# Row maxima added by ScalarE and GpSimd in two attention blocks, and a causal mask added by VectorE in a third

## The reference, cut to what matters

```python
# L1_attn: multi-query, causal; one key/value head of width 16 for all 16 query heads
scores = einsum('bqhd,bkd->bhqk', q, k) / 16 ** 0.5
scores = where(triu(ones(s, s), k=1), -inf, scores)
out = einsum('bhqk,bkd->bqhd', softmax(scores), v) @ o_w.T + o_b
# L2_attn: causal, head width 128
logits = einsum('bthd,bThd->bhtT', q, k) * rsqrt(128)
logits = logits - 1e10 * (1 - (i >= j))
out = (softmax(logits) @ v).reshape(B, T, 2048) @ w_o + b_o
# L2_xattn: head width 16, q against 240 keys of the context and, apart, against 16 more
ctx = _attn(q, k, v) + _attn(q, k_dca, v_dca)
```

## Time and profile before

| | us |
|---|---|
| median of 3 runs | 2208.23 |
| the profiled execution | 2212.03 |
| its span, first to last instruction | 2210.0 |
| TensorE (PE) busy | 1885.6 (85%) |
| VectorE (DVE) busy | 1228.7 (56%) |
| ScalarE (ACT) busy | 787.7 (36%) |
| GpSimd (POOL) busy | 258.7 (12%) |
| mean granted TensorE clock | 0.917 of full speed |

### The profile page before, as it was taken

The page is one execution under the profiler, slowest core; times in us unless marked ns, Lnnn a source line. Parts: engine busy times, 40 slices in busy tenths (PEclk is TensorE's granted clock), DMA queues, the critical chain, the costliest instruction groups (busy, mean ns, idle before and its releaser), DMA issues.

```text
span 2210.0 us, 25454 instructions
## 1 busy us (share of the span) xinstructions
PE 1885.6 (85%) x9078; PEld 1198.9 (54%) x9078; DVE 1228.7 (56%) x2789; ACT 787.7 (36%) x1864; POOL 258.7 (12%) x244
## 2 busy tenths in 40 slices
PE   5684776988669599999898678999998899998698
PEld 3451222555555366666665445555555577777355
DVE  5738998746664444444476685333334666665221
ACT  4215444302342133333344322333333455554111
POOL 2711000000104300000000200000000322220111
PEclk9796877989869799999989889999999999999799
DMA  3001000000442200000000213000002000002210
GB/s 149 1 5 53 0 0 20 1 29 1 188 188 89 96 1 1 1 1 0 4 36 1 100 54 134 0 1 1 0 1 102 15 1 1 1 1 96 85 34 13
DMA packets 17371, 83.13 MB, mean 38 GB/s; under 512 B 3136, under 2 KB 10052, under 8 KB 13152
## 3 DMA queue, kind: packets, MB, share of 16 engines
q1 hardware_dynamic: 11168, 71.35, 8.2%
q0 software_dynamic: 2944, 8.03, 1.2%
q10 hardware_dynamic: 3136, 2.13, 0.3%
HBM read 73.23 MB, written 8.81 MB: 37 GB/s over the span
## 4 chain that ended last, share of the span: by engine, by line
PE 72%; DVE 16%; issue 6%; ACT 3%; POOL 3%; DMA 1%; POOLq 0%; DVEq 0%; SPq 0%; ACTq 0%
PE bank L136 58%; PE bank L141 8%; PE bank L3535 4%; DVE space L795 2%; PE bank L3557 2%; DVE space L784 2%; DVE space L1369 1%; DVE space L3049 1%; DMA space<-in_L_attn 1%; DVE space L178 1%; POOL space L625 1%; POOL space L639 1%; DVE space L272 0%; DVE space L189 0%; ACT space L1551 0%
## 5 line engine op out<-in xcount | busy, mean ns | idle before, releaser
L136 PE MATMUL bank<-space 128*128 128x256 f32 (+16 forms) x6734 | 1453.8, 417 | 73.7 <-ACT space L822 10.3
L136 PEld LDWEIGHTS bank<-space 128*128 128x128 f32 (+7 forms) x6734 | 886.2, 178 | 593.8 <-issue 394.1
L141 PE MATMUL bank<-consts,space 128*128 128x128 f32 (+1 forms) x1602 | 253.5, 299 | 170.7 <-DVE space L189 50.0
L141 PEld LDWEIGHTS bank<-consts,space 128*128 128x128 f32 (+1 forms) x1602 | 201.8, 153 | 236.8 <-issue 123.6
L136 PE MATMUL bank<-space,consts 128*128 128x512 f32 (+2 forms) x150 | 96.2, 769 | 58.5 <-DVE space L790 49.0
L197 POOL TENSOR_TENSOR space<-space,consts 128x4 f32<-128x4 f32 x22 | 24.9, 1132 | 684.8 <-DVE space L184 684.8
L2633 POOL TENSOR_TENSOR space<-space,consts 128x4 f32<-128x4 f32 x64 | 68.6, 1071 | 218.2 <-DVE space L2564 218.2
L2428 ACT ACTIVATE space<-bank,space 128x256 f32<-128x256 f32 x128 | 59.5, 470 | 95.7 <-DVE space L2382 95.7
L2382 DVE TENSOR_REDUCE space<-bank 128x2 f32<-128x512 f32 x64 | 44.1, 688 | 86.9 <-PE bank L136 86.8
L136 PEld LDWEIGHTS bank<-space,consts 128*128 128x128 f32 (+1 forms) x150 | 30.2, 227 | 104.1 <-DVE space L790 70.4
L3535 PE MATMUL bank<-space 128*128 x176 | 80.7, 603 | 3.1 <-DVE space L3685 1.6
(11 more groups left out here) (350 smaller groups left out, 1948.3 us busy)
## 6 DMA issues: line engine op xcount, KB each, us to landing
space<-in_L_ffn SPq DMA_DIRECT2D x13, 2048.0 KB, 11.9
space<-in_L_attn SPq DMA_DIRECT2D x10, 2048.0 KB, 13.4
space<-in_L_xattn SPq DMA_DIRECT2D x4, 2048.0 KB, 10.0
expert_results<-space SPq DMA_DIRECT2D x16, 128.0 KB, 3.6
space<-expert_results SPq DMA_DIRECT2D x8, 256.0 KB, 4.7
space<-in_L_xattn SPq DMA_DIRECT2D x1, 1919.0 KB, 19.8
space<-in_L_xattn SPq DMA_DIRECT2D x1, 1536.0 KB, 6.2
space<-in_L_attn SPq DMA_DIRECT2D x1, 1074.5 KB, 4.9
```

The source lines that it names most:

```text
L136: return self.nc.tensor.matmul(out, lhsT, rhs, start=first, stop=last, skip_group_check=True)
L141: return self.nc.tensor.transpose(out, src, eye)
```

## The change

In the pass of maxima of both `MultiQuery` and `TwoContexts`, the adds of batches 0, 1 and 2 leave VectorE. ScalarE copies each of the two turned banks into a buffer `spare` in `space` and signals `row_kept`; GpSimd adds the buffer to the queries and signals `q_done`. A turn bank is free once it is copied. ScalarE waits with the next batch's copies until GpSimd has added the last one's. The last batch's adds stay with VectorE under a signal of their own, `last_q_done`, which the first mixing product now waits for instead of all of `q_done`. In `Causal` the mask product goes; the two score products now begin their own sums; and VectorE adds the mask to the two diagonal blocks in PSUM ahead of the two row maxima, with a wait between.

```diff
-    def mask_rows(self, bank):
-        out = bank.rearrange("p (a b) -> p a b", b=P)[:, 0::3, :]
-        return self.mm(out, self.ident_bf, repeat(self.mask_bf, 2), True, False)
...
 class MultiQuery(Stage):
...
-            e.wait_ge(*(self.s.maxed(4 * at + j + 1) if kind == "scores" else self.s.q_done(at + 1)))
+            e.wait_ge(*(self.s.maxed(4 * at + j + 1) if kind == "scores" else self.s.row_kept(2 * at + j + 1)))
...
-            if kind == "turn":
-                b = u
-                e.wait_ge(*s.rows_turned(b + 1))
+            if kind == "turn" and u == B - 1:
+                e.wait_ge(*s.rows_turned.all)
...
-                done.then_inc(*s.q_done.one)
+                done.then_inc(*s.last_q_done.one)
...
     def scalar(self, e):
...
+        for b in range(B - 1):
+            e.wait_ge(*s.rows_turned(b + 1))
+            if b >= 1:
+                e.wait_ge(*s.q_done(b))
+            for m in range(2):
+                nc.scalar.activation(self.spare[m], self.bank("turn", b, m), ACT.Copy).then_inc(*s.row_kept.one)
...
     def gpsimd(self, e):
         self.norm.gpsimd(e)
+        for b in range(B - 1):
+            for m in range(2):
+                q = self.q[:, 2 * m:2 * m + 2, b * S:(b + 1) * S]
+                e.wait_ge(*self.s.row_kept(2 * b + m + 1))
+                done = self.c.nc.gpsimd.tensor_tensor(q, q, self.spare[m].rearrange("p (a b) -> p a b", b=S), ALU.add)
+            done.then_inc(*self.s.q_done.one)
...
 class Causal(Heads):
-                c.mask_rows(bank)
                 for i in range(TPB):
                     n = (i + 1) * P
                     done = c.mm(bank[:, i * S:i * S + n], q[:, b2 * S + i * P:b2 * S + (i + 1) * P],
-                                k[:, b2 * S:b2 * S + n], False, True)
+                                k[:, b2 * S:b2 * S + n])
...
+                diagonal = bk[2 + p % 2].rearrange("p (a b) -> p a b", b=P)[:, 0::3, :]
                 e.wait_ge(*s.scores(p + 1))
+                nc.vector.tensor_tensor(diagonal, diagonal, repeat(c.mask_bf, 2), ALU.add).then_inc(*c.v.next())
+                e.wait_ge(*c.v.so_far)
```

More of the change, by code:

```diff
@@ L66 @@
     SPACE = 49600
-    SIGNALS = 52
+    SIGNALS = 54
     def __init__(self, nc, ctx, dram):
@@ L1201, in __init__ @@
         self.rows_ = c.bufs(2, TPB, 4 * P)
-        self.pT = c.bufs(3, 4, 3 * P)
+        self.pT, self.spare = c.bufs(3, 4, 3 * P), c.bufs(2, HALF)
         self.raw, self.inverse = c.sb(4, TOK), c.sb(NT, 16)
@@ L1207, in __init__ @@
             qb_ready=1, k_mm=2, k_ready=2, v_mm=1, v_ready=1, q_mm=8, q_by_vector=4, q_by_scalar=4, scores=16, maxed=64,
-            rows_ready=B, rows_turned=B, q_done=B, st_mm=16, exped=64, mixed=16, raw_ready=16, back=NT, o_ready=NT)
+            rows_ready=B, rows_turned=B, q_done=B - 1, last_q_done=1, row_kept=2 * B - 2, st_mm=16, exped=64, mixed=16, raw_ready=16, back=NT, o_ready=NT)
     def tensor(self, e):
@@ L1295, in scores_turned @@
         if f == 0:
-            e.wait_ge(*s.q_done(b + 1))
+            e.wait_ge(*(s.q_done(b + 1) if b < B - 1 else s.last_q_done.all))
         if u == 0:
@@ L1316, in mix @@
         if u == 0:
-            e.wait_ge(*s.q_done.all)
+            e.wait_ge(*s.last_q_done.all)
         if u >= 1:
@@ L1356, in vector @@
         for kind, u in self.FIRST:
-            if kind == "turn":
-                b = u
-                e.wait_ge(*s.rows_turned(b + 1))
+            if kind == "turn" and u == B - 1:
+                e.wait_ge(*s.rows_turned.all)
                 for m in range(2):
-                    q = self.q[:, 2 * m:2 * m + 2, b * S:(b + 1) * S]
-                    done = nc.vector.tensor_tensor(q, q, self.bank("turn", b, m).rearrange("p (a b) -> p a b", b=S), ALU.add)
-                done.then_inc(*s.q_done.one)
-            else:
+                    q = self.q[:, 2 * m:2 * m + 2, u * S:(u + 1) * S]
+                    done = nc.vector.tensor_tensor(q, q, self.bank("turn", u, m).rearrange("p (a b) -> p a b", b=S), ALU.add)
+                done.then_inc(*s.last_q_done.one)
+            if kind == "scores":
                 b, f = self.UNITS[u]
@@ L2691, in __init__ @@
         self.kd = c.sb(B, self.W4, 4 * DCA)
-        self.many = c.sb(B, P)
+        self.many, self.spare = c.sb(B, P), c.bufs(2, HALF)
         self.rows_ = c.bufs(2, TPB, 4 * P)
@@ L2710, in __init__ @@
             scores=64, maxed=64, late_mm=8, late_tile=8, v_mm=4, v_ready=4, dca_turned=1, dca_ready=1, vd_mm=2, vd_ready=2,
-            bias_mm=1, bias_ready=1, rows_turned=B, q_done=B, st_mm=16, exped=64, mixed=16, raw_ready=16, use=uses,
+            bias_mm=1, bias_ready=1, rows_turned=B, q_done=B - 1, last_q_done=1, row_kept=2 * B - 2, st_mm=16, exped=64, mixed=16, raw_ready=16, use=uses,
             taken=uses, second_exp=B, second_ready=B, o_ready=NT)
@@ L2816, in wait_bank @@
         elif kind == "turn":
-            e.wait_ge(*t.q_done(at + 1))
+            e.wait_ge(*t.row_kept(2 * at + j + 1))
         elif kind == "keys":
@@ L2897, in scores_turned @@
         if f == 0:
-            e.wait_ge(*t.q_done(b + 1))
+            e.wait_ge(*(t.q_done(b + 1) if b < B - 1 else t.last_q_done.all))
         for j in range(4):
@@ L2914, in mix @@
         if u == 0:
-            e.wait_ge(*t.q_done.all)
+            e.wait_ge(*t.last_q_done.all)
             e.wait_ge(*t.v_ready.all)
@@ L3027, in maxima @@
         for kind, at in self.FIRST:
-            if kind == "turn":
-                e.wait_ge(*t.rows_turned(at + 1))
+            if kind == "turn" and at == B - 1:
+                e.wait_ge(*t.rows_turned.all)
                 for m in range(2):
@@ L3032, in maxima @@
                     done = nc.vector.tensor_tensor(q, q, self.bank("turn", at, m).rearrange("p (a b) -> p a b", b=S), ALU.add)
-                done.then_inc(*t.q_done.one)
+                done.then_inc(*t.last_q_done.one)
             elif kind == "second_values":
@@ L3145, in scalar @@
         for kind, at in self.FIRST:
-            if kind not in ("scores", "turn"):
+            if kind == "turn" and at < B - 1:
+                e.wait_ge(*t.rows_turned(at + 1))
+                if at >= 1:
+                    e.wait_ge(*t.q_done(at))
+                for m in range(2):
+                    nc.scalar.activation(self.spare[m], self.bank(kind, at, m), ACT.Copy).then_inc(*t.row_kept.one)
+            elif kind not in ("scores", "turn"):
                 self.take_beside(e, kind, at, self.bank(kind, at, 0))
@@ L3192, in gpsimd @@
         done.then_inc(*s.rows_clear.one)
+        for b in range(B - 1):
+            for m in range(2):
+                q = self.q[:, 2 * m:2 * m + 2, b * S:(b + 1) * S]
+                e.wait_ge(*t.row_kept(2 * b + m + 1))
+                done = nc.gpsimd.tensor_tensor(q, q, self.spare[m].rearrange("p (a b) -> p a b", b=S), ALU.add)
+            done.then_inc(*t.q_done.one)
         n = 0
```

## The result

The changed kernel takes 2197.67 us (median of 6 runs, 2195.58 to 2198.94) against 2209.28 for the kernel before beside it: ratio 0.9946, 95% interval 0.9934 to 0.9959, or 11.6 us faster. The forecast was 2197.1. The profiled execution took 2198.28 us; its span of 2196.3 us is 13.7 us shorter than the one of before.

A forecast was written before the change was run, and what follows sets the result against it. VectorE was taken to bound both passes of maxima, TensorE the causal block. Gains of 5.65 + 2.4 + 3.1 = 11.15 us, off the median 2208.23, gave 2197.1 us, range 2192.5 to 2204.5.

The forecast's parts named there:

- Mask product, 64 x 0.11 us on the chain of every step: Causal block: removing 64 mask products from TensorE's list, 0.11 us each, was to gain 7.0 us.
- The add's price and its cover: Causal block: VectorE's mask add delays by 0.45 us (upper end 0.72), hidden in all but the last three transposing steps.
- The slack of 0.56 us: Causal block, plain odd steps: normalising ends 0.56 us before the transposes' operand load, so 0.45 fits with 0.11 to spare.
- Last three steps: Causal block's last three transposing steps: no projection hides the add, costing 3 x 0.45 = 1.35 us; waits 1.4 instead of 0.93.
- Multi-query pass, what is late next: Multi-query pass: TensorE is late next, so each turn gains 1.19 - 0.4 = 0.8 us, three turns 2.4 us.
- the ring: Multi-query pass: two turn banks shift bank reuse by two, so the next unit awaits the previous unit's second maximum; VectorE idles 0.36 us.
- Second context: Second context's pass of maxima: three turns without VectorE's adds gain 0.7, 1.19 and 1.19 us, in sum 3.1 us.
- Rival 1: Engine behind takes most: causal add 0.68 us, giving 2202.2; with passes gaining nothing too, 2207.7; chance 0.15 for both strengths.
- Rival 2: Passes of maxima: 12 new GpSimd adds block VectorE 1.27 us each, 15.2 us in all, giving 2212.3; chance 0.04.
- Rival 3: Passes: longer TensorE gaps halve its clock, about 0.5 us for each of 32 units, 16 us, giving 2213; chance 0.02.
- I let the clock stand: Causal block: TensorE stays as dense as before, so its granted clock of 1.00 was assumed unchanged.

## Why the prediction was right

- **Mask product, 64 x 0.11 us on the chain of every step.** Right. The causal stretch lost 5.42 us net, and 5.42 + 3 x 0.47 is 6.8, or 0.107 us per product.
- **The add's price and its cover.** 0.43 us and a hand-over to 0.46 or 0.47, where 0.45 was taken by the row of the same width. The slack of 0.56 us was real: 0.10 is left, the kernel without any add shows nothing paid in plain steps, and the doubled add shows the price once the slack is gone (10.0 us).
- **Last three steps.** 1.40 us of wait each, as forecast.
- **Multi-query pass, what is late next.** 0.42 us of each 1.19 handed back to TensorE; 2.26 us against 2.4. The split turn shows that the ring was the reason.
- **Second context.** Gaps of 0.53, 0 and 0 us against 0.5, 0 and 0: 2.98 us against 3.1.
- **Rival 1** fell with the 0.43 us record. **Rival 2** fell for the maxima (median 0.547 us), but GpSimd's adds do hold up small instructions between operands in `space`; the forecast never asked where the adds lie against those. They clear them by 2.8 us. **Rival 3** fell too: both passes ran at a clock of 1.00.
- **The step that failed is a side one: "I let the clock stand".** Within the block it stood at 1.00. Behind it, the longer waits of the last three steps went with one fall of the clock instead of two, worth 4.8 us in profiles. Behind the multi-query pass 5.0 us were gained, behind the second context's 6.5 lost (1033.6 instead of 1027.0), and 0.2 lost ahead of the first pass. Their sum, 3.0 us gained, is the difference between 10.7 by stretches and 13.7 by spans. The two large ones aren't scatter: behind the second context's pass the kernel before took 1027.04 and 1027.05 us in its two profiles, the changed kernel 1033.45 to 1034.08 in its four, and every other kernel 1030.0 or more; behind the multi-query pass the changed kernel took 238.1 to 238.6 in all four, the kernel before 243.4 in both, though two kernels with the pass as before and another causal block took 239.5 and 239.6. So the changed kernel's profiles differ from those of before by microseconds, in both directions, in stretches whose work the change leaves as it was, and the forecast had no term for that. Why this is so stays open. That the median came out 0.6 us from the forecast is therefore partly luck; what is shown is the 10.7, in profiles, and in whole times a gain in three comparisons of four.

## What to carry to other kernels

Before giving work to another engine, measure the slack of the receiving chain in the timeline, per kind of step, from the common start to the moment at which the bounding engine asks: here 0.56 us in the tightest kind of step let an add of 0.47 us vanish in 61 of 64 steps, and the next 0.47 us cost 10 us. When the bounding engine of a ring of buffers is relieved, look at which buffer the following unit reuses; a turn of two banks took back a third of the gain, and two turns of one bank each didn't. And check the ends of a pipelined loop separately, where the cover is missing. Don't take the agreement of a whole time with a sum of stretches as proof of the sum: here stretches without any edit moved by 4.8, 5.0 and 6.5 us.

## What the runs showed of the hardware that was not expected

**TensorE's granted clock behind a block went with the waits inside it in most profiles, not in all.** By length and mean clock of the stretch, between the causal block and the next pass it fell to half twice in the four profiles with a mask product and waits of 0.93 us in the last steps (44.01 to 44.05 us), and once in seven of the nine with longer waits (39.20 to 39.22 us). The other two of the nine took 40.8 and 50.6 us, and the kernel with neither product nor add, whose waits are 0.93 us too, 40.5. So the waits alone don't settle it. In the changed kernel, ahead of the pass, the clock at half and back at full:

```profile
1094.00:1098.00 4.00, 4.00 (x8) 1.98 (x8) 3.58 (x15) 3.71 (x5) 2.00 (x3) 0.50 0.86 354
1100.00:1110.00 10.00, 10.00 (x33) 4.78 (x32) 5.91 (x15) 5.85 (x12) 0.51 (x1) 1.00 0.00 0
```

and the second fall in the kernel before, over work that the changed kernel does from 1103.5 to about 1108.7, inside the second row above:

```profile
1116.00:1126.00 10.00, 10.00 (x20) 4.96 (x20) 5.12 (x12) 3.62 (x9) 0.00 (x0) 0.50 0.00 0
```

What took some 5 us at full clock takes 10 at half; ScalarE waits for the products, 3.34 us at the longest, and VectorE for ScalarE.

**A running GpSimd add held up a tiny VectorE instruction for up to 1.08 us** when its operands lay in `space`, and the maxima, which read PSUM, not at all (0.54 us).

**A VectorE add from PSUM to PSUM** with 256 columns takes 0.43 us, 0.02 more than one into `space` (0.41).
